# First layer's heads: the dense products of a slot stand between its scores and its turns

## The chip, the cores and the metric

One core of one Trainium2 chip runs the whole program. The metric is the device time of one execution in microseconds (us), the median of several runs. TensorE (PE) does the matrix products and the transposes; its weight loads are listed apart as PEld. VectorE (DVE), ScalarE (ACT) and GpSimd (POOL) do the rest, and SyncE (SP) issues transfers.

## The reference, cut to what matters

Four layers, each an attention part and a feed-forward part that both read the layer's normalised input. Only the attention of the first layer is touched. It has two batches of 1024 tokens, 16 query heads of 128 dimensions and 4 groups of keys and values, and it is causal:

```python
q = einsum('bsh,he->bse', x, w_q).reshape(b, sq, GROUPS, HPG, KVC)
scores = einsum('bqgpd,bkgd->bgqpk', q, k) * SCALE
scores = where(causal, scores, -inf)
probs = softmax(scores, axis=-1)
ctx = einsum('bgqpk,bkgd->bqgpd', probs, v).reshape(b, sq, HEADS * KVC)
return einsum('bse,eh->bsh', ctx, w_dense)
```

## The kernel before, in words

The function `l0_heads` runs the 16 heads one after the other, the inner ones in a hardware loop. Each engine has its own instruction list, written out by hand, and works through it in that order; the lists meet only at semaphores. Nothing plans the order: it is that of the calls in each engine's `step`.

The work of a head is 16 units. A unit is one tile of 128 queries (number t, 0 to 7, of batch b), whose scores are 128 x 128(t+1). In each batch the tiles come in the order t = 0, 1, 6, 7, 2, 3, 4, 5. Two units that follow each other are a pair. A head is 18 slots: 16 for units and two in which the queries of a coming head are projected. In a batch's half of a head these are nine slots: t=0, 1, 6, 7, then the projection, then t=2, 3, 4, 5.

A unit passes through the engines over several slots:

- its own slot: TensorE makes the scores (`scores`, L486 to L488 and the causal mask at L490) in a PSUM bank pair `sc`; DVE takes the row maximum (`row_max`, L592); ACT takes the exponential (`exp`, L682) and writes `probs`.
- two slots later: TensorE turns the probabilities (`turn_probs`, L501: transposes of 128 x 128 blocks, t+1 of them, four to a tile, two PSUM banks `tp` in turn); ACT writes the rounded high part (`high_probs`, L672, tile PTH); DVE writes the remainder (`low_probs`, L614, tile PTL).
- three slots after the pair's second unit: TensorE weighs the values (`weigh_values`, L516 to L518, into `cx`), and ACT copies the result to `ctxT` (`keep_ctx`, L690).
- four slots after the pair's second unit: TensorE multiplies `ctxT` with the output weights (`dense`, L530, plain fp32, two products that the trace shows as four records, into `outp`), and DVE adds it to the sum (`add_dense`, L624).

So a slot of TensorE's list holds scores, then turns of the unit two slots back, then, in some slots, a dense product or the weighing of values. A slot never has both a dense product and a weighing. The slots with a dense product are those of t=1, t=7, t=2 and t=4; what they turn is t=5 (six blocks), t=1 (two blocks), t=7 (eight blocks) and t=2 (three blocks). The slot after each of them has no dense product.

What TensorE waits for, by name: the turns wait for the probabilities and for a free bank (`pt_lo`, the remainder of the tile two before: `pe.wait_ge(pt_lo, NT * h + n - 1)`, L499); the weighing waits for the remainder of all its unit's tiles (`pt_lo`, L509); the dense product waits for `ctx_ready`, the copy of the context (L526), and for the sum before it (`added`, L528). ACT's list in a slot is `high_probs`, then `exp` (or `high_queries` in a projection slot), then `keep_ctx`. DVE's list in a slot is `row_max`, then `invert` and `low_probs`, then `low_queries` in a projection slot, then `add_dense`.

The two lines that set the order of a slot on TensorE after its scores:

```python
if u := unit_at(h, s, 2):
    turn_probs(*u)
if (u := unit_at(h, s, 4)) and u[1] % 2:
    dense(*u)
```

Of the kernel before, what the change touches and what calls it, by code (L numbers as in the profile page):

```python
# [217 lines left out]
def split_product(pe, out, w_hi, w_lo, x_hi, x_lo):  # L218

    terms = [(w, x, c) for c in range(DC) for w, x in ((w_hi, x_hi), (w_hi, x_lo), (w_lo, x_hi))]  # L220
    for i, (w, x, c) in enumerate(terms):
        mm = pe.matmul(out, w(c), x(c), start=(i == 0), stop=(i == len(terms) - 1))  # L222
    return mm
# [142 lines left out]
def l0_heads(nc, k, a, kd, vd, kv):  # L366
# [15 lines left out]
    with Stage(nc, "l0h") as st:  # L382
# [20 lines left out]
        def back(h, s, n):  # L403

            return (h, s - n) if s >= n else (h - 1, s - n + NS)

        def exists(h):
            return not isinstance(h, int) or 0 <= h <= LAST

        def unit_at(h, s, n):  # L410


            hh, ss = back(h, s, n)
            kind, i = SLOTS[ss]
            return (hh, i) if kind == "unit" and exists(hh) else None
# [12 lines left out]
        with nc.Block() as block:  # L428
# [29 lines left out]
            def _(pe):  # L458
                def project(h, b, bank):

                    pe.wait_ge(wlo_ready, h + 1)
                    for j in range(S // BANK):
                        tok = slice(b * S + j * BANK, b * S + (j + 1) * BANK)
                        mm = split_product(pe, bank[:, j * BANK:(j + 1) * BANK], lambda c: wq_hi[:, c, :], lambda c: wq_lo[:, c, :],
                                           lambda c: k.XH[:, c, tok], lambda c: k.XL[:, c, tok])
                        mm.then_inc(q_made, 1)

                def bank_free(h, s):
                    hh, ss = back(h, s, 2)
                    if exists(hh):  # L470
                        kind, i = SLOTS[ss]
                        if kind == "unit":
                            pe.wait_ge(probs_ready, NU * hh + i + 1)
                        elif exists(hh + 1 - i):
                            pe.wait_ge(ql_ready, 2 * hh + (3 if i == 0 else 2))

                def scores(h, s, i):
                    b, t = UNITS[i]
                    pe.wait_ge(kv.keys_here[b], h + 1)
                    pe.wait_ge(ql_ready, 2 * h + 1 + b)  # L480
                    q = slice(b * S + t * P, b * S + (t + 1) * P)
                    for lo in range(0, (t + 1) * P, BANK):
                        n = min(BANK, (t + 1) * P - lo)
                        key = slice(b * S + lo, b * S + lo + n)
                        diagonal = lo + n == (t + 1) * P
                        pe.matmul(sc[s % 2][:, lo:lo + n], QH[:, q], kv.KH[:, key], start=True, stop=False)  # L486
                        pe.matmul(sc[s % 2][:, lo:lo + n], QH[:, q], kv.KL[:, key], start=False, stop=False)
                        mm = pe.matmul(sc[s % 2][:, lo:lo + n], QL[:, q], kv.KH[:, key], start=False, stop=not diagonal)  # L488
                        if diagonal:
                            mm = pe.matmul(sc[s % 2][:, t * P:(t + 1) * P], ident[:, :], causal[:, :], start=False, stop=True)  # L490
                    mm.then_inc(scores_ready, 1)

                def turn_probs(h, i):
                    b, t = UNITS[i]
                    pe.wait_ge(probs_ready, NU * h + i + 1)
                    for j in range(TILES[i]):
                        n = FIRST_TILE[i] + j
                        if n >= 2 or not isinstance(h, int) or h > 0:
                            pe.wait_ge(pt_lo, NT * h + n - 1)  # L499
                        for kb in range(4 * j, min(4 * j + 4, t + 1)):  # L500
                            mm = pe.transpose(tp[n % 2][:, (kb - 4 * j) * P:(kb - 4 * j + 1) * P], probs[:, i % 4, kb * P:(kb + 1) * P], k.ident[:, :])  # L501
                        mm.then_inc(turned, 1)

                def weigh_values(h, i):


                    b, t = UNITS[i]
                    pair = i // 2
                    pe.wait_ge(pt_lo, NT * h + FIRST_TILE[i + 1])  # L509
                    pe.wait_ge(kv.values_here[b], h + 1)  # L510
                    if pair or not isinstance(h, int) or h > 0:
                        pe.wait_ge(ctx_ready, NPAIR * h + pair)
                    for kb in range(t + 1):
                        col = slice(0 if kb < t else P, L0_PAIR)
                        V = b * NQ + kb
                        pe.matmul(cx[:, col], kv.VH[:, V, :], PTH[:, pair % 2, kb, col], start=(kb == 0), stop=False)  # L516
                        pe.matmul(cx[:, col], kv.VH[:, V, :], PTL[:, pair % 2, kb, col], start=False, stop=False)  # L517
                        mm = pe.matmul(cx[:, col], kv.VL[:, V, :], PTH[:, pair % 2, kb, col], start=False, stop=(kb == t))  # L518
                    mm.then_inc(pv_done, 1)

                def dense(h, i):

                    pair = i // 2
                    if pair == 0:
                        pe.wait_ge(wd_loaded, 16)
                    pe.wait_ge(ctx_ready, NPAIR * h + pair + 1)  # L526
                    if pair or not isinstance(h, int) or h > 0:
                        pe.wait_ge(added, NPAIR * h + pair)  # L528
                    for j in range(2):
                        mm = pe.matmul(outp[:, j * D:(j + 1) * D], ctxT[:, pair % 2, j * P:(j + 1) * P],  # L530
                                       wd[:, ds(h, 1), :].rearrange("p a n -> p (a n)"), start=True, stop=True)
                    mm.then_inc(dense_done, 1)

                def step(h, s):
                    if exists(h):
                        kind, i = SLOTS[s]
                        if kind == "unit":
                            bank_free(h, s)
                            scores(h, s, i)
                        elif exists(h + 1 - i):  # L540
                            bank_free(h, s)
                            project(h + 1 - i, i, sc[s % 2])
                    if u := unit_at(h, s, 2):
                        turn_probs(*u)
                    if (u := unit_at(h, s, 4)) and u[1] % 2:
                        dense(*u)
                    if (u := unit_at(h, s, 3)) and u[1] % 2:
                        weigh_values(*u)

                project(0, 0, sc[1])  # L550
                pe.wait_ge(mask_here, 1)
                steps(pe, step)
                for n in range(NJ * DC):
                    j, c = divmod(n, DC)
# [2427 lines left out]
```

## Time and profile before

| | us |
|---|---|
| median of 3 runs | 3763.67 (3762.89 to 3767.64) |
| the profiled execution's own time | 3760.89 |
| its span in the trace | 3759.1 |
| TensorE busy | 3383.6 (90%) |
| DVE busy | 2424.6 (64%) |
| ACT busy | 1569.3 (42%) |
| the stage of the heads, about | 120 to 968 |

The stage of the heads takes 848 us of the span, about 52 us for a head and 26 us for a batch's half of one. The groups of instructions say what each line costs in sum; the waits say who waited for whom; the timeline of one engine in one short stretch says in which order the instructions ran, when each started, how long its record is, and in brackets how long the engine sat idle before it and what released it. A matmul's record includes the drain of its result, so records overlap: the distance from one start to the next is what a matmul occupies.

### The profile page before, as it was taken

How to read it: one execution, taken by the hardware profiler on the slowest of the kernel's cores; microseconds unless marked ns; L12 is line 12 of the kernel's file. 1: busy time of each engine (PE TensorE's matmuls, PEld its weight loads, DVE VectorE, ACT ScalarE, POOL GpSimd, SP SyncE). 2: the span in 40 equal slices, each digit the busy share in tenths (PEclk: the TensorE clock that was granted, in tenths of full speed). 3: DMA queues.
4: the chain of work that ended last, by engine and by line, in shares of the span. 5: the costliest groups of instructions: out<-in, count | busy, mean ns of one | idle time of the engine just before them, and what ended most of it. 6: DMA issues, size and time to landing. Idle time of an engine off the chain costs nothing. (4 is left out here: it accounts for less than half of the span.)

```text
span 3759.1 us, 65234 instructions
## 1 busy us (share of the span) xinstructions
PE 3383.6 (90%) x21360; PEld 2613.8 (70%) x21360; DVE 2424.6 (64%) x4499; ACT 1569.3 (42%) x2871; POOL 1181.3 (31%) x851
## 2 busy tenths in 40 slices
PE   6799999999697999999996669999769999799997
PEld 4688888888475888888883335555348887388883
DVE  3466666666424656656655778888468887488873
ACT  2355555555233444444442316666333332333332
POOL 1202020110024666666662400000014444444444
PEclk8899999999898999999998879999979999899998
DMA  3100000000101000000000502222044443144441
GB/s 111 63 3 25 3 24 3 18 10 0 35 0 45 15 18 18 16 18 18 18 8 3 199 36 82 82 82 74 12 137 117 112 114 80 44 107 116 114 98 48
DMA packets 133296, 199.97 MB, mean 53 GB/s; under 512 B 23072, under 2 KB 78240, under 8 KB 132896
## 3 DMA queue, kind: packets, MB, share of 16 engines
q1 hardware_dynamic: 127072, 190.55, 16.3%
q0 software_dynamic: 6144, 8.39, 1.4%
q8 instruction: 45, 0.74, 0.1%
q14 instruction: 35, 0.29, 0.0%
HBM read 162.06 MB, written 36.57 MB: 53 GB/s over the span
## 5 line engine op out<-in xcount | busy, mean ns | idle before, releaser
L1942 DVE TENSOR_REDUCE l2h_half<-l2h_s 128x1 f32<-128x512 f32 x512 | 337.5, 686 | 50.3 <-PE l2h_s L1844 49.3
L1929 ACT ACTIVATE l2h_PT<-l2h_s 128x1024 f32<-128x1024 f32 x256 | 248.3, 1022 | 164.9 <-PE l2h_s L1854 164.8
L592 DVE TENSOR_REDUCE l0h_negtop<-l0h_sc 128x1 f32<-128x128 f32 (+7 forms) x256 | 192.8, 753 | 191.7 <-PE l0h_sc L490 187.8
L614 DVE TENSOR_TENSOR l0h_PTL<-l0h_tp,l0h_PTH 128x512 fp32r<-128x512 f32 (+3 forms) x384 | 200.4, 549 | 122.9 <-ACT l0h_PTH L672 120.0
L672 ACT ACTIVATE l0h_PTH<-l0h_tp 128x512 fp32r<-128x512 f32 (+3 forms) x384 | 175.4, 496 | 219.1 <-PE l0h_tp L501 218.9
L1844 PE MATMUL l2h_s<-l2h_K,l2h_Q 128*128 128x512 f32 x512 | 219.1, 466 | 23.5 <-DMA l2h_K<-l_split 20.4
L682 ACT ACTIVATE l0h_probs<-l0h_sc,l0h_negtop 128x128 f32<-128x128 f32 (+7 forms) x256 | 190.3, 743 | 116.1 <-DVE l0h_negtop L592 115.1
L159 POOL TENSOR_TENSOR XN<-XN,n_rstd 128x512 f32<-128x512 f32 x32 | 39.9, 1268 | 593.7 <-DVE n_rstd L140 593.7
L568 POOL TENSOR_TENSOR l0h_wq_lo<-l0h_wq,l0h_wq_hi 128x256 fp32r<-128x256 f32 x16 | 11.8, 739 | 630.0 <-ACT l0h_wq_hi L656 630.0
L516 PE MATMUL l0h_cx<-l0h_PTH,l0a_VH 128*128 128x256 f32 (+1 forms) x640 | 184.3, 288 | 17.0 <-DVE l0h_PTL L614 16.9
L501 PE MATMUL l0h_tp<-ident,l0h_probs 128*128 128x128 f32 x1152 | 177.4, 276 | 20.7 <-DVE l0h_PTL L614 20.7
L517 PE MATMUL l0h_cx<-l0h_PTL,l0a_VH 128*128 128x256 f32 (+1 forms) x640 | 180.0, 281 | 0.0
L518 PE MATMUL l0h_cx<-l0h_PTH,l0a_VL 128*128 128x256 f32 (+1 forms) x640 | 179.5, 280 | 0.0
L1844 PEld LDWEIGHTS l2h_s<-l2h_K,l2h_Q 128*128 128x128 f32 x512 | 99.2, 195 | 113.9 <-DVE l2h_half L1942 75.3
L1854 PE MATMUL l2h_s<-l2h_Q,l2h_K 128*128 128x512 f32 x512 | 162.3, 400 | 0.0
L1138 ACT ACTIVATE l1a_kswap<-l1a_pk,l1a_bias 64x512 f32<-64x512 f32 x64 | 43.8, 685 | 278.0 <-PE l1a_pk L222 278.0
L2587 POOL TENSOR_TENSOR l3p_w_lo<-l3p_w,l3p_w_hi 128x1024 fp32r<-128x1024 f32 x34 | 80.4, 2363 | 252.1 <-ACT l3p_w_hi L2530 252.1
L486 PE MATMUL l0h_sc<-l0a_KH,l0h_QH 128*128 128x512 f32 (+3 forms) x384 | 156.9, 409 | 2.0 <-DVE l0h_QL L598 1.5
L2673 DVE TENSOR_TENSOR_SCAN l3p_table<-l3p_decb,l3p_eye 128x512 f32<-128x512 f32 x128 | 151.2, 1222 | 0.4 <-issue 0.4
L2711 DVE SCALAR_TENSOR_TENSOR l3p_state<-l3p_state,l3p_prow,l3p_dsm 128x128 f32<-128x128 f32 x192 | 146.1, 761 | 6.8
L501 PEld LDWEIGHTS l0h_tp<-ident,l0h_probs 128*128 128x128 f32 x1152 | 126.5, 141 | 34.2 <-DVE l0h_PTL L614 28.2
L2538 ACT ACTIVATE l3p_xT<-l3p_px 128x512 f32<-128x512 f32 x64 | 38.3, 598 | 263.4 <-PE l3p_px L222 263.4
(423 smaller groups left out, 9903.8 us busy)
## 6 DMA issues: line engine op xcount, KB each, us to landing
l3p_decb<-l_decays SPq DMA_DIRECT2D x128, 256.0 KB, 4.4
l3p_w<-L_w SPq DMA_DIRECT2D x34, 512.0 KB, 3.6
l2h_Q<-l_split SPq DMA_DIRECT2D x64, 256.0 KB
l2h_K<-l_split SPq DMA_DIRECT2D x64, 256.0 KB
l3p_prow<-l_decays SPq DMA_DIRECT2D x128, 128.0 KB, 3.1
l_split<-l2q_hi SPq DMA_DIRECT2D x16, 512.0 KB, 3.9
l_split<-l2q_lo SPq DMA_DIRECT2D x16, 512.0 KB, 3.8
l3p_wgu<-L_ffn_w_gate_up SPq DMA_DIRECT2D x32, 256.0 KB, 4.8
```

Source lines behind the costliest of these rows:

```text
L501: mm = pe.transpose(tp[n % 2][:, (kb - 4 * j) * P:(kb - 4 * j + 1) * P], probs[:, i % 4, kb * P:(kb + 1) * P], k.ident[:, :])
L516: pe.matmul(cx[:, col], kv.VH[:, V, :], PTH[:, pair % 2, kb, col], start=(kb == 0), stop=False)
L517: pe.matmul(cx[:, col], kv.VH[:, V, :], PTL[:, pair % 2, kb, col], start=False, stop=False)
L518: mm = pe.matmul(cx[:, col], kv.VL[:, V, :], PTH[:, pair % 2, kb, col], start=False, stop=(kb == t))
L592: dve.reduce_max(negtop[:, i % 4:i % 4 + 1], sc[s % 2][:, 0:(t + 1) * P], AX_X, negate=True).then_inc(top_ready, 1)
L614: dve.tensor_tensor(PTL[part], tp[n % 2][:, 0:m * P].rearrange("p (m n) -> p m n", m=m), PTH[part].bitcast(F32), ALU.subtract).then_inc(pt ...
L672: act.activation(PTH[:, pair % 2, 4 * j:4 * j + m, i % 2 * P:(i % 2 + 1) * P], tp[n % 2][:, 0:m * P].rearrange("p (m n) -> p m n", m=m), A ...
L682: act.activation(probs[:, i % 4, 0:(t + 1) * P], sc[s % 2][:, 0:(t + 1) * P], ACT.Exp, bias=negtop[:, i % 4:i % 4 + 1], accum_out=total[:, ...
L1844: pe.matmul(bank(slot_of(i))[:, :], Q1[:, b, t * P:(t + 1) * P], K1[:, b, z * BANK:(z + 1) * BANK], start=True, stop=True).then_inc(s1_mad ...
L1854: mm = pe.matmul(s2[kb % 2][:, z * BANK:(z + 1) * BANK], K2[:, b, kb * P:(kb + 1) * P], Q2[:, b, z * BANK:(z + 1) * BANK], start=True, sto ...
L1929: act.activation(PT[:, b, kb, :], s2[kb % 2][:, :], ACT.Exp, scale=L2_SCALE).then_inc(exped, 1)
L1942: dve.reduce_max(half[:, b, t, z:z + 1], bank(slot_of(i))[:, :], AX_X).then_inc(s1_read, 1)
```

## The change

Two statements of TensorE's `step` change places. In a slot that has a dense product, it now comes right behind the slot's scores, and the turns come behind it. No instruction is added or taken away, and the lists of DVE, ACT, GpSimd and SyncE are the same as before, word for word.

```diff
@@ -540,10 +540,10 @@
                         elif exists(h + 1 - i):
                             bank_free(h, s)
                             project(h + 1 - i, i, sc[s % 2])
+                    if (u := unit_at(h, s, 4)) and u[1] % 2:
+                        dense(*u)
                     if u := unit_at(h, s, 2):
                         turn_probs(*u)
-                    if (u := unit_at(h, s, 4)) and u[1] % 2:
-                        dense(*u)
                     if (u := unit_at(h, s, 3)) and u[1] % 2:
                         weigh_values(*u)
```

TensorE, the slot of t=2, whose turns are the eight blocks of t=7 (names: `l0h_sc` the scores' bank, `l0h_tp` the turns' bank, `l0h_outp` the dense product's bank; a leading + is a row of the changed kernel, a leading - one of the kernel before):

```order
 L488 MATMUL l0h_sc<-l0a_KH,l0h_QL 128x384
 L490 MATMUL l0h_sc<-l0h_causal,l0h_ident 128x128
+L530 MATMUL l0h_outp<-l0h_wd,l0h_ctxT 128x256 x2
 L501 MATMUL l0h_tp<-ident,l0h_probs 128x128 x8
-L530 MATMUL l0h_outp<-l0h_wd,l0h_ctxT 128x256 x2
 L486 MATMUL l0h_sc<-l0a_KH,l0h_QH 128x512
```

The eight turns now stand behind the dense product and directly ahead of the scores of t=3, after which the values of t=7 are weighed.

TensorE, the slot of t=4, whose turns are the three blocks of t=2:

```order
 L488 MATMUL l0h_sc<-l0a_KH,l0h_QL 128x128
 L490 MATMUL l0h_sc<-l0h_causal,l0h_ident 128x128
+L530 MATMUL l0h_outp<-l0h_wd,l0h_ctxT 128x256 x2
 L501 MATMUL l0h_tp<-ident,l0h_probs 128x128 x3
-L530 MATMUL l0h_outp<-l0h_wd,l0h_ctxT 128x256 x2
 L486 MATMUL l0h_sc<-l0a_KH,l0h_QH 128x512
```

The three turns moved behind the dense product; what follows them is the slot of t=5.

TensorE, the slot of t=1, whose turns are the six blocks of t=5:

```order
 L488 MATMUL l0h_sc<-l0a_KH,l0h_QL 128x256
 L490 MATMUL l0h_sc<-l0h_causal,l0h_ident 128x128
+L530 MATMUL l0h_outp<-l0h_wd,l0h_ctxT 128x256 x2
 L501 MATMUL l0h_tp<-ident,l0h_probs 128x128 x6
-L530 MATMUL l0h_outp<-l0h_wd,l0h_ctxT 128x256 x2
 L486 MATMUL l0h_sc<-l0a_KH,l0h_QH 128x512
```

Between the weighing that makes the dense product's input and the dense product there now stand only the scores of t=1.

## Rows read from the trace of the kernel before

**Rows 1.** Page: busy time of the engines over the whole span.
```profile
PE 3383.6 (90%) x21360; PEld 2613.8 (70%) x21360; DVE 2424.6 (64%) x4499; ACT 1569.3 (42%) x2871; POOL 1181.3 (31%) x851
```
**Rows 2.** Busy time by stretch: PE, PEld, DVE, ACT, POOL, granted clock, DMA share, GB/s.
```profile
120.00:968.00 848.00, 806.93 (x5401) 707.42 (x5400) 526.27 (x1093) 453.46 (x1104) 68.38 (x39) 1.00 0.03 11
```
**Rows 3.** Waits of PE, 120 to 968: us in total, times, longest us.
```profile
PE l0h_tp L501 <- DVE l0h_PTL L614: 20.7, 34, 1.0
PE l0h_cx L516 <- DVE l0h_PTL L614: 16.9, 32, 0.7
```
**Rows 4.** Waits of PE's weight loads, same stretch.
```profile
PEld l0h_cx L516 <- DVE l0h_PTL L614: 21.6, 32, 1.1
```
**Rows 5.** Timeline of PE, slots of t=7 to t=3: start, length, instruction, idle before.
```profile
417.77 0.39 PE L501 MATMUL l0h_tp<-ident,l0h_probs 128*128 128x128 f32 x2
...
422.28 0.36 PE L516 MATMUL l0h_cx<-l0h_PTH,l0a_VH 128*128 128x256 f32 x1
...
423.66 1.08 PE L501 MATMUL l0h_tp<-ident,l0h_probs 128*128 128x128 f32 x8
424.57 1.08 PE L530 MATMUL l0h_outp<-l0h_wd,l0h_ctxT 128*128 x4
...
426.99 0.39 PE L516 MATMUL l0h_cx<-l0h_PTH,l0a_VH 128*128 128x256 f32 x1 [0.56 <-DVE l0h_PTL L614]
```
**Rows 6.** Timeline of ACT, around the slot of t=2.
```profile
424.06 0.42 ACT L690 ACTIVATE l0h_ctxT<-l0h_cx 128x256 f32<-128x256 f32 x1
424.32 1.13 ACT L672 ACTIVATE l0h_PTH<-l0h_tp 128x512 fp32r<-128x512 f32 x2
```
**Rows 7.** Timeline of DVE, slot of t=2.
```profile
425.67 1.26 DVE L614 TENSOR_TENSOR l0h_PTL<-l0h_tp,l0h_PTH 128x512 fp32r<-128x512 f32 x2
```
**Rows 8.** Timeline of PE, slots of t=4 to t=0.
```profile
430.99 0.50 PE L501 MATMUL l0h_tp<-ident,l0h_probs 128*128 128x128 f32 x3
431.32 1.03 PE L530 MATMUL l0h_outp<-l0h_wd,l0h_ctxT 128*128 x4
432.00 0.58 PE L486 MATMUL l0h_sc<-l0a_KH,l0h_QH 128*128 128x512 f32 x1
...
435.33 0.33 PE L501 MATMUL l0h_tp<-ident,l0h_probs 128*128 128x128 f32 x1 [0.61 <-DVE l0h_PTL L614]
```
**Rows 9.** Timeline of ACT, slots of t=4 to t=1.
```profile
431.52 0.49 ACT L672 ACTIVATE l0h_PTH<-l0h_tp 128x384 fp32r<-128x384 f32 x1 [1.05 <-PE l0h_tp L501]
...
437.25 0.38 ACT L690 ACTIVATE l0h_ctxT<-l0h_cx 128x256 f32<-128x256 f32 x1 [0.76 <-PE l0h_cx L518]
438.09 0.87 ACT L672 ACTIVATE l0h_PTH<-l0h_tp 128x512 fp32r<-128x512 f32 x2 [0.46 <-PE l0h_tp L501]
```
**Rows 10.** Timeline of DVE, slots of t=4 to t=1.
```profile
432.04 0.56 DVE L614 TENSOR_TENSOR l0h_PTL<-l0h_tp,l0h_PTH 128x384 fp32r<-128x384 f32 x1
432.52 0.86 DVE L624 SCALAR_TENSOR_TENSOR l0h_acc<-l0h_outp,l0h_inv,l0h_acc 128x256 f32<-128x256 f32 x2
433.51 0.96 DVE L592 TENSOR_REDUCE l0h_negtop<-l0h_sc 128x1 f32<-128x768 f32 x1
434.38 0.15 DVE L605 RECIPROCAL l0h_inv<-l0h_total 128x2 f32<-128x2 f32 x1
434.58 0.69 DVE L614 TENSOR_TENSOR l0h_PTL<-l0h_tp,l0h_PTH 128x512 fp32r<-128x512 f32 x1
...
438.72 1.02 DVE L614 TENSOR_TENSOR l0h_PTL<-l0h_tp,l0h_PTH 128x512 fp32r<-128x512 f32 x2 [0.58 <-ACT l0h_PTH L672]
```
**Rows 11.** Timeline of PE, slots of t=1 and t=6.
```profile
437.45 0.83 PE L501 MATMUL l0h_tp<-ident,l0h_probs 128*128 128x128 f32 x6
...
440.30 0.36 PE L516 MATMUL l0h_cx<-l0h_PTH,l0a_VH 128*128 128x256 f32 x1
```
**Rows 12.** Timeline of PE in the last head, where turns follow a dense product directly.
```profile
940.82 1.03 PE L530 MATMUL l0h_outp<-l0h_wd,l0h_ctxT 128*128 128x256 f32 x4
941.68 0.60 PE L501 MATMUL l0h_tp<-ident,l0h_probs 128*128 128x128 f32 x4
```

## The prediction, made before the changed kernel was run

> **What bounds the kernel now.** I read the page's busy times first: TensorE is busy for 90% of the span, the next engine for 64% [rows 1]. Then the stage of the heads alone, the only one that the change touches: of 848.0 us TensorE's records cover 806.9, at a granted clock of 1.00, its 2.4 GHz level; DVE works 526.3 us, ACT 453.5 [rows 2]. So the stage ends when TensorE ends, and each us that TensorE waits there is a us of the kernel. Third, the waits: two groups carry nearly all of them, and both are for DVE's remainders of the turned probabilities: 20.7 us in 34 waits ahead of a turn, 16.9 in 32 ahead of a weighing [rows 3]. There are 32 half heads, so each wait comes once in a half. Last, the timelines of three engines over one half (848 / 32, about 26 us) show where. Wait A, 0.56 us, stands ahead of the weighing of t=7, in the slot of t=3 [rows 5]. Wait B, 0.61 us, stands ahead of the second tile of t=4's turns, in the slot of t=0 [rows 8]. Neither slot holds a dense product, so the change cannot lay a dense product over either wait. What it does is start four turns per half later, and ask for four dense inputs earlier.
>
> **What a dense product costs where it stands.** Before, the scores behind it start 0.68 us later (431.32 to 432.00 [rows 8]), but the one place in this trace where turns follow it directly, late in the last head, shows 0.86 us (940.82 to 941.68 [rows 12]). I take 0.86 as the delay of the turns and 0.68 as the lower bound. I count no change in the stream's sum: the same products run, only the neighbours change. That part is bounded below.
>
> **First place, the slot of t=2.** Ahead stands a projection slot, in which ACT's list has the rounding of the queries and only then the copy of the context: that copy starts at 424.06 and lasts 0.42, so `ctxT` is there at 424.48 [rows 6]. TensorE is through with the scores at 423.66 and starts the eight turns there; before, these covered the copy, and the dense product at 424.57 found its input ready [rows 5]. Now the dense product is asked for at 423.66 and stands some 0.87 us. Then the chain runs: dense starts at about 424.55 (the copy's end plus 0.06, the lag between DVE's end at 425.67 + 1.26 = 426.93 [rows 7] and TensorE's start at 426.99 [rows 5]), turns at 424.55 + 0.86 = 425.41, ACT's high part 0.64 later (437.45 to 438.09 [rows 9, 11]) at 426.05, DVE's remainder 0.63 later (438.09 to 438.72 [rows 9, 10]) at 426.68. DVE is free by then, since before it began this same work at 425.67 [rows 7]. The pair of remainders takes 1.16 us when ACT's pieces (1.13 for two [rows 6]) pace it, my estimate from that row, so it ends at 427.84 and the weighing of t=7 starts at 427.90 instead of 426.99: **+0.91 us**. Wait A stays about as long as it is (turns and scores are later by as much), and a new wait on `ctxT` of about 0.87 stands ahead of the dense product. With 0.68 for the dense product it is +0.73. Behind the waiting dense product TensorE's list holds the turns and the scores of t=3; ACT's next high part and DVE's next remainder wait for these.
>
> **Second place, the slot of t=4.** The dense product finds its input here: the five pieces of scores in between are long. The three turns start at 430.99 + 0.86 = 431.85 instead of 430.99 [rows 8]. ACT followed 0.53 later (431.52 [rows 9]): now 432.38. DVE followed ACT by 0.52 (432.04 [rows 10]): now 432.90. From there DVE's list goes on without a pause: the addition of the dense product 0.48 later (432.04 to 432.52), the next row maximum 0.78 after that (its 0.86 less the overlap of 0.08 that neighbours on DVE show), at 434.16 instead of 433.51; the reciprocal 0.87 on (433.51 to 434.38), at 435.03; the remainder of t=3 about 0.07 on, at 435.10 instead of 434.58 [rows 10]. That remainder is what wait B waits for, so B grows by **+0.52 us**. The cover here was 0.21 of pause ahead of the row maximum and 0.13 ahead of the remainder; 0.86 less these is the same 0.52. With 0.68 it is +0.34.
>
> **Third place, the slot of t=1.** The weighing of t=3 has just ended, and only the short scores of t=1 stand ahead of the dense product. ACT's copy starts at 437.25 and ends at 437.63 [rows 9], so the product starts at 437.69, not at 437.45: a new wait of 0.24. The six turns of t=5 start at 438.55 instead of 437.45 [rows 11], 1.10 later. ACT and DVE had idled ahead of them [rows 9, 10], so the chain moves one to one: remainders at 438.72 + 1.10 = 439.82, done after 1.02 [rows 10] at 440.84, weighing of t=5 at 440.90 instead of 440.30 [rows 11]: **+0.60 us**; at least the +0.24 of the first wait, if the rest were hidden. With 0.68, +0.42.
>
> **Fourth place, the slot of t=7.** The turns of t=1 (two blocks) are followed by a projection before the values are weighed: 4.51 us from the turns at 417.77 to the weighing at 422.28 [rows 5], where the chain from the turns to the remainder needs about 0.64 + 0.63 and the remainder itself. Cost zero; the projection is the cover. Without it the price would be the 0.86 at most.
>
> **The rule weighed.** TensorE's weight loads show no load that passed a waiting product: the loads of the weighing waited for the remainders too, 21.6 us in 32 waits [rows 4], though their weights, the values, do not depend on these. So I count no load of the turns as done during the new waits. The Trainium skill, TensorE: Matmul & The Clock Gate, section The mechanism, says that TensorE pulls weight loads ahead of matmuls in flight. By that the first load of the turns could lie in the new wait of the first and third place; at an estimated 0.1 us each (a turn's spacing of 0.91/8) the sum would be some 6 us smaller. The trace rather speaks against it here.
>
> **The sum.** 0.91 + 0.52 + 0.60 = 2.03 us for a half. I count 31 halves: the first half head lacks a third place, and the last half of the last head has no projection ahead of its first. 31 x 2.03 = 63 us. Against the profiled execution, 3760.9 us, that gives 3824; the median of the runs is 2.8 higher, so 3763.7 + 63 = 3827 us. Bounds: with 0.68 for the dense product 0.73 + 0.34 + 0.42 = 1.49, or 46 us, 3810; above, a slot that loses another 0.05 where neighbours changed (four per half, 128 in all) adds 6 us, 3833. The same 0.05 below zero would take 6 off.
>
> **Rivals.**
> - *Only the first place costs.* If the lists of ACT and DVE hide the second and third (0.13 + 0.21 of pause at the second, the scores of t=6 at the third), 31 x 0.91 = 28 us remain: 3792. For it: the third place has the scores of t=6 between turns and weighing. Against: the weighing already starts at 440.30 with DVE done at 439.74, 0.56 of slack against 1.10. Chance 0.10.
> - *Faster.* A dense product is dear for what follows: the next scores start at 0.68, but turns at 0.86, so the product's tail lies on its successor. If turns, whose loads are short, cover 0.13 of that tail better than scores do, TensorE's stream shrinks by 128 x 0.13 = 17 us: 3747. It decides only if the three places together cost less than 4 x 0.13 = 0.52 us a half; I count 2.03, and rows 12 show no such cover. Chance 0.04.
> - *No change.* The dense product could be asked for early without delay if its input were always there, and the turns' delay fall into waits A and B: 3764. Against: the copy's end at 424.48 stands 0.82 behind 423.66. Chance 0.03.
> - *Dearer.* If the late exponentials also hold back the score banks (that of t=4 stands behind the late high part on ACT, and the scores of t=0 want its bank), or ACT's copies fall behind, another 0.4 us a half: 3840. Chance 0.06.
>
> **The numbers.** The forecast has 0.77; its own range is 3810 to 3833. The range from 3792 to 3836 takes in the first rival and leaves out the other three, 0.13. A difference under 0.2% (7.5 us) is about what a measurement can't tell from none. Slower by more: 0.77 + 0.10 + 0.06 = 0.93; within: 0.03; faster: 0.04.
>
> **What would show it.** In the trace after: waits of TensorE for ACT's `ctxT`, near 0.87 us ahead of the dense product of the slot of t=2 and near 0.24 in that of t=1, 35 us in all, where before there was next to none; waits ahead of t=4's second tile of turns near 1.13 instead of 0.61, about 36 us in all; waits ahead of the weighing not shorter than 16.9 and up by some 11 (the third place's 0.36). The stage near 911 us instead of 848. Nothing else may move. I am wrong if the turns start earlier than 0.7 us behind the dense product, or if the waits for `ctxT` are missing.

## The result and the profile after

The changed kernel takes 3846.82 us (median, 3842.23 to 3848.37) against 3765.65 for the kernel before in the same runs: a ratio of 1.021, with a 95% interval of 1.0193 to 1.0228. It is slower by 81 us. The prediction had 3827 us, slower by 63, with a range up to 3836: the sign, the three places and their order of size were right, but the sum was too small by 18 us, and the time lies 11 us above the range. One execution of the kernel before in a later group of runs (4480.49 us, at a mean granted clock of 0.72 where the others have 0.95) is left out of every comparison.

Nearly all of the time went in the stage of the heads: 80.2 us there, as measured below, of the 81 between the medians. The page's first part and the stage's row of busy time by stretch (columns as in [rows 2]):

```profile
PE 3418.4 (89%) x21360; PEld 2626.0 (68%) x21360; DVE 2424.4 (63%) x4499; ACT 1563.1 (41%) x2871; POOL 1183.1 (31%) x851
120.00:1052.00 932.00, 839.95 (x5408) 718.58 (x5407) 528.05 (x1096) 446.45 (x1104) 68.18 (x39) 1.00 0.03 10
```

The same instructions ran, the granted clock stayed at 1.00, the 2.4 GHz level, and DVE's and ACT's work in the stage is the same within 7 us. TensorE's records cover 33 us more (839.95 against 806.93), though the products are the same. Most of that is waiting out of sight: a record includes the drain, so a wait that begins under the record before it is counted as idle only from that record's end. Against [rows 3], TensorE's waits in the stage (us in total, times, longest):

```profile
PE l0h_tp L501 <- DVE l0h_PTL L614: 32.3, 33, 1.5
PE l0h_cx L516 <- DVE l0h_PTL L614: 27.4, 33, 1.6
PE l0h_outp L530 <- ACT l0h_ctxT L690: 26.0, 46, 0.8
```

Both old waits grew (20.7 to 32.3 and 16.9 to 27.4), and a third appeared, of the dense product for the copy of the context. These rows add up to 48 us more than before; with the 33 us under records that is about what the stage lost.

One half head of the changed kernel, in the order of time. TensorE's timeline (start, length, instruction, idle before), to be laid beside [rows 5, 8, 11]:

```profile
452.00 0.39 PE L486 MATMUL l0h_sc<-l0a_KH,l0h_QH 128*128 128x384 f32 x1
...
453.51 1.13 PE L530 MATMUL l0h_outp<-l0h_wd,l0h_ctxT 128*128 x4 [0.71 <-ACT l0h_ctxT L690]
454.48 1.04 PE L501 MATMUL l0h_tp<-ident,l0h_probs 128*128 128x128 f32 x8
...
457.09 0.38 PE L516 MATMUL l0h_cx<-l0h_PTH,l0a_VH 128*128 128x256 f32 x1 [0.80 <-DVE l0h_PTL L614]
...
461.08 1.08 PE L530 MATMUL l0h_outp<-l0h_wd,l0h_ctxT 128*128 x4
462.00 0.49 PE L501 MATMUL l0h_tp<-ident,l0h_probs 128*128 128x128 f32 x3
...
465.98 0.33 PE L501 MATMUL l0h_tp<-ident,l0h_probs 128*128 128x128 f32 x1 [0.84 <-DVE l0h_PTL L614]
...
468.03 0.23 PE L490 MATMUL l0h_sc<-l0h_causal,l0h_ident 128*128 128x128 bf16 x1
468.43 1.12 PE L530 MATMUL l0h_outp<-l0h_wd,l0h_ctxT 128*128 x4 [0.17 <-ACT l0h_ctxT L690]
469.39 0.82 PE L501 MATMUL l0h_tp<-ident,l0h_probs 128*128 128x128 f32 x6
...
471.41 0.33 PE L501 MATMUL l0h_tp<-ident,l0h_probs 128*128 128x128 f32 x1
471.74 0.39 PE L516 MATMUL l0h_cx<-l0h_PTH,l0a_VH 128*128 128x256 f32 x1
```

ACT's timeline in the same half, to be laid beside [rows 6, 9]:

```profile
453.04 0.41 ACT L690 ACTIVATE l0h_ctxT<-l0h_cx 128x256 f32<-128x256 f32 x1
455.12 1.09 ACT L672 ACTIVATE l0h_PTH<-l0h_tp 128x512 fp32r<-128x512 f32 x2 [1.66 <-PE l0h_tp L501]
...
467.90 0.39 ACT L690 ACTIVATE l0h_ctxT<-l0h_cx 128x256 f32<-128x256 f32 x1 [0.61 <-PE l0h_cx L518]
```

And DVE's, beside [rows 7, 10]:

```profile
455.75 1.29 DVE L614 TENSOR_TENSOR l0h_PTL<-l0h_tp,l0h_PTH 128x512 fp32r<-128x512 f32 x2 [1.00 <-ACT l0h_PTH L672]
...
465.25 0.67 DVE L614 TENSOR_TENSOR l0h_PTL<-l0h_tp,l0h_PTH 128x512 fp32r<-128x512 f32 x1
...
470.66 1.02 DVE L614 TENSOR_TENSOR l0h_PTL<-l0h_tp,l0h_PTH 128x512 fp32r<-128x512 f32 x2 [1.87 <-ACT l0h_PTH L672]
```

Slot of t=2: the copy ends at 453.04 + 0.41 = 453.45, the dense product starts at 453.51, the turns only at 454.48; DVE, which before was late itself, now idles 1.00 us until ACT has a high part for it. From the first score of t=2 to the weighing of t=7 it is 457.09 - 452.00 = 5.09 us. Slot of t=4: the product needs no wait, the turns start 0.92 behind it, and t=4's second tile of turns waits until 465.98 for a remainder that DVE starts at 465.25. Slot of t=1: the copy starts at 467.90, the dense product at 468.43, the turns at 469.39, the weighing of t=5 at 471.74. The product could have followed the mask's product (468.03) by some 0.06, so it waits 0.34 us, of which the timeline shows the 0.17 behind that record's end.

### The profile page after: what moved, and what is told of

Its sections match the earlier page's. It is cut to its first block and busy times, and to the rows that moved or that the text cites. A ratio compares the mean times of both kernels' runs of the same rounds, so it can differ in the third digit from the quotient of the medians.

```text
span 3845.1 us, 65234 instructions
## 1 busy us (share of the span) xinstructions
PE 3418.4 (89%) x21360; PEld 2626.0 (68%) x21360; DVE 2424.4 (63%) x4499; ACT 1563.1 (41%) x2871; POOL 1183.1 (31%) x851
## 5 line engine op out<-in xcount | busy, mean ns | idle before, releaser
L516 PE MATMUL l0h_cx<-l0h_PTH,l0a_VH 128*128 128x256 f32 (+1 forms) x640 | 185.0, 289 | 27.5 <-DVE l0h_PTL L614 27.4
L501 PE MATMUL l0h_tp<-ident,l0h_probs 128*128 128x128 f32 x1152 | 176.8, 276 | 32.5 <-DVE l0h_PTL L614 32.3
L501 PEld LDWEIGHTS l0h_tp<-ident,l0h_probs 128*128 128x128 f32 x1152 | 136.7, 141 | 58.6 <-DVE l0h_PTL L614 40.1
L530 PE MATMUL l0h_outp<-l0h_wd,l0h_ctxT 128*128 (+1 forms) x512 | 141.5, 399 | 26.9 <-ACT l0h_ctxT L690 26.0
L486 PE MATMUL l0h_sc<-l0a_KH,l0h_QH 128*128 128x512 f32 (+3 forms) x384 | 147.6, 384 | 2.1 <-DVE l0h_QL L598 1.5
```

## The experiments

The stage below is measured from the first scores of the first head to the start of the last addition of a dense product, so that what lies ahead of the heads does not enter. For the kernel before these are 124.67 and 964.1, 839.4 us; for the changed one 126.05 and 1045.6, 919.6 us: +80.2. "Over before" is the difference of the medians within the runs that share their runs of the kernel before. The stage is read from one traced execution of each kernel, so the two columns can differ by some us.

| kernel | median | over before | ratio, 95% | stage over before |
|---|---|---|---|---|
| changed | 3846.82 | +81.2 | 1.0193 to 1.0228 | +80.2 |
| only in the slot of t=2 | 3807.97 | +41.3 | 1.0089 to 1.0123 | +36.4 |
| only in the slot of t=4 | 3780.84 | +14.2 | 1.0032 to 1.0068 | +17.9 |
| only in the slot of t=1 | 3794.97 | +28.3 | 1.0054 to 1.0088 | +24.9 |
| only in the slot of t=7 | 3767.14 | +0.5 | 0.9995 to 1.0015 | +2.0 |
| changed, without the context's wait | 3809.07 | +40.3 | 1.0088 to 1.0122 | +45.9 |
| changed, copy ahead of the queries | 3819.28 | +50.5 | 1.0118 to 1.0152 | +52.8 |
| changed, addition one slot later | 3832.87 | +64.1 | 1.0151 to 1.0185 | +63.7 |
| before, dense product of t=4 in the slot of t=0 | 3752.97 | -15.8 | 0.9951 to 0.9976 | -14.6 |
| before, DVE exchanged in the slot of t=2 | 3750.31 | -14.1 | 0.9950 to 0.9972 | -14.7 |
| changed, DVE exchanged in the slot of t=2 | 3845.56 | +81.2 | 1.0197 to 1.0230 | +80.1 |
| before, both of these | 3735.67 | -28.7 | 0.9903 to 0.9931 | -29.1 |

**One place at a time.** Two theories: each place pays for itself, through the waits that the prediction followed; or a dense product is simply dearer in the stream behind scores than behind turns, which would cost alike in all four slots. The edit, here for the slot of t=2 (slots 5 and 14; the others are 7 and 16, 1 and 10, 3 and 12):

```diff
+                    early = s in (5, 14)
+                    if early and (u := unit_at(h, s, 4)) and u[1] % 2:
+                        dense(*u)
                     if u := unit_at(h, s, 2):
                         turn_probs(*u)
-                    if (u := unit_at(h, s, 4)) and u[1] % 2:
+                    if not early and (u := unit_at(h, s, 4)) and u[1] % 2:
                         dense(*u)
```

> The dense product ahead of the turns only in the slot of t=2, the other three slots as before. Theory of waits (each place pays for itself, by the wait on the context's copy and the later chain): the trace after shows 5.09 us from the scores of t=2 to the weighing of t=7 against 3.99 before, so +1.1 a half, 31 halves: +34 us, stage of the heads about 882. The prediction's own size was +28. Rival, a dearer stream (a dense product costs more behind scores than behind turns, alike in all four slots): a quarter of 81, +20.

> Only in the slot of t=4. Theory of waits: DVE's list (remainder of t=2, addition, row maximum, remainder of t=3) moves, and the wait ahead of t=4's second tile of turns grows by 0.52 to 0.55: 32 halves, +17 us, no new wait on the context. Rival, a dearer stream: +20, and it would show between the dense product and the scores of t=5, not at the second tile.

> Only in the slot of t=1. Theory of waits: +0.6 (the prediction) to +0.8 (read from the trace after) a half: +19 to +25 us; a wait on the context's copy of 0.2 to 0.4 ahead of the dense product and a new wait ahead of the weighing of t=5. Rival, a dearer stream: +20 with no wait ahead of the weighing.

> Only in the slot of t=7, where a projection follows the turns. Theory of waits: 0 to +3 us (the trace after shows 0.05 to 0.09 a half). Rival, a dearer stream: +20, as in the others. This run tells the two apart.

The four stages add up to 36.4 + 17.9 + 24.9 + 2.0 = 81.2 us, against 80.2 for the whole change (the medians to 84.3, against 81.2). They are unlike, and the fourth, where only the neighbours change and a projection covers the rest, costs 2.0 us of the stage, 0.06 a half, and nothing that the medians can tell. So a dense product that costs alike in all four slots is out, and so is the rival that the first place alone would cost. TensorE's waits, in the kernel with the slot of t=2 alone, then with t=4 alone, then with t=1 alone:

```profile
PE l0h_cx L516 <- DVE l0h_PTL L617: 26.6, 33, 0.9
PE l0h_outp L530 <- ACT l0h_ctxT L693: 23.2, 32, 0.8
PE l0h_tp L501 <- DVE l0h_PTL L617: 20.4, 33, 1.0
```

```profile
PE l0h_tp L501 <- DVE l0h_PTL L617: 32.5, 34, 1.5
PE l0h_cx L516 <- DVE l0h_PTL L617: 17.2, 32, 0.7
```

```profile
PE l0h_cx L516 <- DVE l0h_PTL L617: 18.0, 32, 1.6
PE l0h_outp L530 <- ACT l0h_ctxT L693: 3.4, 16, 0.5
```

With t=2 alone, the wait for the copy and the growth of the wait ahead of the weighing are there, and the turns' wait is as before. With t=4 alone it is the turns' wait that grows, by 12 us in 34 waits, and nothing new waits for the context.

With t=1 alone, the new wait ahead of the weighing of t=5 that was expected is not in the list (18.0 us against 16.9 before), and no wait there is what the rival had said of this slot. The timelines of the changed kernel tell more. Ahead of that weighing stands a single turn, and the weighing starts 0.33 us behind it (471.41 to 471.74); in the kernel before it was 0.04 (440.26 below, to 440.30 [rows 11]):

```profile
440.26 0.28 PE L501 MATMUL l0h_tp<-ident,l0h_probs 128*128 128x128 f32 x1
```

DVE's remainders end at 470.66 + 1.02 = 471.68, and the weighing follows 0.06 later. So there is a wait of 0.29, and the turn's record of 0.33 hides all of it. The kernel with t=1 alone has the same 0.33.

**The wait for the context taken away.** In the changed kernel the dense product reads the identity, which is always there:

```diff
-                    pe.wait_ge(ctx_ready, NPAIR * h + pair + 1)
...
-                        mm = pe.matmul(outp[:, j * D:(j + 1) * D], ctxT[:, pair % 2, j * P:(j + 1) * P],
+                        mm = pe.matmul(outp[:, j * D:(j + 1) * D], k.ident[:, :],
```

> The changed kernel, but the dense product takes the identity in place of the context as its stationary operand and does not wait for the copy (so the attention's result is left out). Theory of waits: the waits for the copy go, and what they delayed: the first place falls from +1.10 to about +0.2 a half, the third from +0.80 to about +0.45, the second stays at +0.55, the fourth at 0.05 to 0.09: 1.3 a half, about +41 us over the kernel before, 40 below the changed one. If the waits for the copy were only a symptom and the later turns alone were the price, little would go: over +65. The start of the turns behind the dense product should fall from 0.97 to 0.92 or less if the context's weight load is what makes the difference.

It is 40.3 us over before, 41 below the changed kernel (the stage: 45.9, 34 below): about half of the loss came from asking for the context too early. The rest comes with the later turns. TensorE's timeline around the slot of t=2:

```profile
440.28 0.39 PE L486 MATMUL l0h_sc<-l0a_KH,l0h_QH 128*128 128x384 f32 x1
...
440.92 1.08 PE L529 MATMUL l0h_outp<-l0h_wd,ident 128*128 x4
441.84 1.04 PE L501 MATMUL l0h_tp<-ident,l0h_probs 128*128 128x128 f32 x8
...
444.52 0.38 PE L516 MATMUL l0h_cx<-l0h_PTH,l0a_VH 128*128 128x256 f32 x1 [0.88 <-DVE l0h_PTL L613]
```

From the scores of t=2 to the weighing it is 4.24 us, 0.85 less than in the changed kernel; and the turns start 0.92 us behind the dense product, not 0.97.

**The copy ahead of the queries.** In the changed kernel, ACT's list of a projection slot:

```diff
                         elif exists(h + 1 - i):
+                            if (u := unit_at(h, s, 3)) and u[1] % 2:
+                                keep_ctx(*u)
                             high_queries(2 * h + (3 if i == 0 else 2), i, sc[s % 2])
```

(with the call at the slot's end left out there)

> The changed kernel, but ACT copies the context ahead of rounding the queries in the two projection slots of a head. Theory of waits: at the first place the copy ends about 0.8 us earlier, the dense product waits 0.1 instead of 0.87; the queries' remainder and with it the row maximum and the remainder of t=7 on DVE come about 0.5 later, so about 0.6 of the 0.8 is gained: 31 halves, 15 to 20 us below the changed kernel, +62 to +66 over before. If ACT's order is not what holds the copy back: no difference to the changed kernel.

It gains 27 us of the stage (31 by the medians), more than the 15 to 20 expected, and the wait for the context falls from 26.0 us in 46 waits to this row:

```profile
PE l0h_outp L530 <- ACT l0h_ctxT L690: 3.4, 16, 0.5
```

So the order of ACT's list is what held the first place's copy back. I had charged the later rounding of the queries with 0.2 us a half on DVE; the trace shows that DVE's remainder of t=7 still starts 0.63 behind ACT's high part (443.45 to 444.08), so that delay is hidden. ACT's timeline there, then DVE's:

```profile
441.41 0.38 ACT L690 ACTIVATE l0h_ctxT<-l0h_cx 128x256 f32<-128x256 f32 x1
...
443.45 1.09 ACT L672 ACTIVATE l0h_PTH<-l0h_tp 128x512 fp32r<-128x512 f32 x2 [0.68 <-PE l0h_tp L501]
```

```profile
444.08 1.29 DVE L614 TENSOR_TENSOR l0h_PTL<-l0h_tp,l0h_PTH 128x512 fp32r<-128x512 f32 x2
```

**The addition one slot later.** In the changed kernel, DVE's list:

```diff
+                    if (u := unit_at(h, s, 5)) and s in (8, 17) and u[1] % 2:
+                        add_dense(*u)
-                    if (u := unit_at(h, s, 4)) and u[1] % 2:
+                    if (u := unit_at(h, s, 4)) and s not in (7, 16) and u[1] % 2:
                         add_dense(*u)
```

> The changed kernel, but DVE adds the dense product of the slot of t=4 one slot later, behind the remainder of t=3. Theory for the second place (the chain runs through DVE's list, whose addition of 0.78 stands ahead of the row maximum): the +0.55 there vanishes, 32 halves: 17 us below the changed kernel. If the chain there runs through ACT instead (high part, exponential, high part): no difference.

The stage falls by 16.5 us, and TensorE's waits ahead of the turns from 32.3 to 16.0 us (the row below, from the waits). So the second place's chain runs through DVE's list, as the prediction had it.

```profile
PE l0h_tp L501 <- DVE l0h_PTL L614: 16.0, 33, 1.0
```

**Can a dense product between scores and turns be worth something?** Where the turns would wait anyway, it should. In the kernel before, on TensorE (and likewise the addition on DVE):

```diff
+                    if (u := unit_at(h, s, 6)) and s in (0, 9) and u[1] % 2:
+                        dense(*u)
                     if u := unit_at(h, s, 2):
                         turn_probs(*u)
-                    if (u := unit_at(h, s, 4)) and u[1] % 2:
+                    if (u := unit_at(h, s, 4)) and s not in (7, 16) and u[1] % 2:
                         dense(*u)
```

> The kernel before, but the dense product of the slot of t=4 is made two slots later on TensorE and DVE, in the slot of t=0 between its scores and its turns. There the wait of 0.61 for the remainder of t=3 stands with nothing to cover it. Theory of waits: the product covers it, the turns' second tile waits no more: 32 x 0.6 = 19 us below the kernel before. If turns that start later always cost by the length of the product: no gain, or up to +10 us.

It is faster than before, by 0.24 to 0.49%, and wait B is gone: 0.7 us in 3 waits are left of 20.7 in 34. The row of the wait, then TensorE's timeline in the slot of t=0:

```profile
PE l0h_tp L501 <- DVE l0h_PTL L616: 0.7, 3, 0.3
```

```profile
428.06 1.08 PE L530 MATMUL l0h_outp<-l0h_wd,l0h_ctxT 128*128 x4
428.98 0.71 PE L501 MATMUL l0h_tp<-ident,l0h_probs 128*128 128x128 f32 x5
```

The five turns of t=4 run in one piece behind the product. This is the order of the change (scores, dense product, turns), in a slot where the turns had to wait anyway and with an input that is long there. The gain is 4 to 5 us less than the wait that it removed. About 4 us of it are lost in the slot of t=1: its turns and its dense product take 0.71 and 0.75 us to the next start (431.35, 432.06, 432.81) instead of 0.66 and 0.68 (437.45, 438.11, 438.79 before), 0.12 a half. What makes them longer was not tried.

**What holds wait A.** DVE's list has the row maximum of t=2 ahead of the remainders of t=7. Exchanged, in the slot of t=2 only:

```diff
-                    if kind == "unit" and exists(h):
+                    if s not in (5, 14) and kind == "unit" and exists(h):
                         row_max(h, s, i)
...
                         low_probs(*u)
+                    if s in (5, 14) and exists(h):
+                        row_max(h, s, i)
```

> The kernel before, but in the slot of t=2 DVE makes the remainders of t=7 ahead of the row maximum of t=2. Wait A ahead of the weighing of t=7 is then held by DVE's list no more: the remainders can start at 425.13 instead of 425.67, so 0.5 of the 0.56 goes: 32 x 0.5 = 16 us below before. If A is set by the turns and ACT instead: no difference.

> The same exchange on DVE, in the changed kernel. There, by the theory of waits, the remainders of t=7 wait for turns that start 1.8 us later and DVE idles 1.0 us ahead of them, so the exchange gives nothing to TensorE: within 3 us of the changed kernel, +80 over before (the row maximum of t=2 comes later, which costs nothing while its bank is not wanted). If DVE's list still set wait A in the changed kernel: 16 us below it.

In the kernel before, the exchange takes 14.1 us off and wait A falls from 16.9 us to 0.7. In the changed kernel it does nothing (+81.2 over before, with it and without), and the wait stays at 27.5: there the remainders wait for the late turns, and DVE idles 1.47 us ahead of them. The same wait, by name and place, has another cause in the two kernels. The rows are the wait ahead of the weighing with the exchange, in the kernel before and then in the changed one, and last the timeline of DVE's remainders in the changed one:

```profile
PE l0h_cx L516 <- DVE l0h_PTL L614: 0.7, 1, 0.7
```

```profile
PE l0h_cx L516 <- DVE l0h_PTL L614: 27.5, 33, 1.6
```

```profile
454.68 1.29 DVE L614 TENSOR_TENSOR l0h_PTL<-l0h_tp,l0h_PTH 128x512 fp32r<-128x512 f32 x2 [1.47 <-ACT l0h_PTH L674]
```

**Both together,** on the kernel before:

> The kernel before with both: the dense product of the slot of t=4 made in the slot of t=0 between scores and turns, and DVE's exchange in the slot of t=2. If the two waits of a half are separate, the gains add: 15 + 16 = 31 us below before, 3735. If one wait only moves to the other: 16.

The gains add: 3735.67 us, ratio 0.9917 (0.9903 to 0.9931). That is 28.7 us, where the two alone give 15.8 + 14.1 = 29.9. It is the fastest of all the kernels here. The two waits of a half head were separate.

## Why the prediction fell short

Right were: that no dense product covers waits A or B; that three of the four slots pay, by the chains named; that the fourth is covered; that ACT's list holds back the first place's copy, and DVE's addition the second place.

Of the waits that it named, the one ahead of the turns came to 32.3 us (about 36 said) and the one for the context to 26.0 (35 said; the trace counts no idle while the records of the scores' last products run out). The one ahead of the weighing came to 27.4, where about 28 was said, but that was luck: the prediction let wait A stay and put the growth into the third place. With t=1 alone the row is 18.0, with t=2 alone 26.6. It was wait A that grew, from 0.56 to 0.80 in the timelines, and the third place's wait is hidden under a record.

What failed is the size of the terms, and first the step "What a dense product costs where it stands": 0.86 us as the delay of the turns. In the half head shown, the four slots cost 1.10, 0.55, 0.80 and 0.05 us, 2.50 in all, where the sum had 0.91, 0.52, 0.60 and 0, 2.03. (Over the 32 halves the mean distances from one weighing to the next grew by 1.14, 0.54, 0.74 and 0.09, also 2.50, 80 us.) Each of the first three begins with the delay of the turns by a dense product, taken as 0.86 from [rows 12]; it measured 0.97 in the first place, 0.92 in the second, 0.96 in the third. That alone is 0.11 + 0.06 + 0.10 = 0.27 of the missing 0.47.

The rest: in the first place the pair of remainders took 1.29 us (455.75) instead of 1.16, which is 0.13. The 1.16 was taken from ACT's pace, but DVE's own work on this pair already took 1.26 before, in [rows 7], with ACT's pieces finished at 424.32 + 1.13 = 425.45, ahead of its start. In the third place the copy's end reached the product after 0.14 instead of 0.06 (467.90 + 0.39 = 468.29, against 468.43), which is 0.08, and the fourth slot's 0.05 (4.56 from 446.71 to 451.27, against 4.51 before) was put at nothing. Smaller differences, as of a copy in the first place that ended 0.03 earlier, take the remaining 0.06 off.

Why 0.86 did not carry over can be read from the weight loads. The rows are the load of the dense product in the last head of the kernel before, then the loads in the first and second place of the changed one:

```profile
940.71 0.73 PEld L530 LDWEIGHTS l0h_outp<-l0h_wd,l0h_ctxT 128*128 128x128 f32 x4
```

```profile
453.51 0.73 PEld L530 LDWEIGHTS l0h_outp<-l0h_wd,l0h_ctxT 128*128 128x128 f32 x4 [0.84 <-ACT l0h_ctxT L690]
454.26 1.01 PEld L501 LDWEIGHTS l0h_tp<-ident,l0h_probs 128*128 128x128 f32 x8
...
461.02 0.74 PEld L530 LDWEIGHTS l0h_outp<-l0h_wd,l0h_ctxT 128*128 128x128 f32 x4
```

In the row that I took the price from, the load began at 940.71, 0.11 us ahead of its product, beneath two turns. Behind the scores it begins 0.06 ahead (461.02 to 461.08), since the mask's product there is short (0.06 to the next start); behind a wait it begins with the product, because the context is the stationary operand and can't be loaded before it exists. Lead and delay add up to 0.97 or 0.98 each time: 0.11 + 0.86, 0.06 + 0.92, 0 + 0.97. The kernel without the wait agrees: 0.92 in the place where the changed kernel has 0.97.

The kernel with the copy ahead of the queries parts the lead from the wait. In its slot of t=2 the product waits no more (it starts 0.07 behind the mask's product at 441.79), but the copy ends only at 441.41 + 0.38 = 441.79, so the load has a lead of just 0.01, and the turns follow after 0.96. Its load, then its product and turns:

```profile
441.85 0.73 PEld L530 LDWEIGHTS l0h_outp<-l0h_wd,l0h_ctxT 128*128 128x128 f32 x4
```

```profile
441.86 1.12 PE L530 MATMUL l0h_outp<-l0h_wd,l0h_ctxT 128*128 x4
442.82 1.04 PE L501 MATMUL l0h_tp<-ident,l0h_probs 128*128 128x128 f32 x8
```

The kernel before showed the same of the scores behind a dense product. In the slot of t=4 the load leads by 0.11 and the scores follow after 0.68 (431.32 to 432.00 [rows 8]); in the slot of t=2 it leads by 0.05 and they follow after 0.74 (424.57 [rows 5] to 425.31). The two loads, then those scores:

```profile
431.21 0.73 PEld L530 LDWEIGHTS l0h_outp<-l0h_wd,l0h_ctxT 128*128 128x128 f32 x4
```

```profile
424.52 0.73 PEld L530 LDWEIGHTS l0h_outp<-l0h_wd,l0h_ctxT 128*128 128x128 f32 x4
```

```profile
425.31 0.58 PE L486 MATMUL l0h_sc<-l0a_KH,l0h_QH 128*128 128x512 f32 x1
```

So the trace before already held a price that moved with the lead. That the uncovered load is the cause is read from these sums; no run was made to vary the lead alone.

The rule of the Trainium skill that was weighed (TensorE: Matmul & The Clock Gate, section The mechanism: loads are pulled ahead of matmuls in flight) was rightly not counted. The turns' first load in the first place comes at 454.26, behind the dense product's at 453.51: no load of the turns passed the waiting product. The changed order even loses the small lead that the rule describes.

The rival "dearer" had a mechanism that did occur: the late exponential of t=4 held back the score bank of t=0, so that in this half 0.62 us (463.45 to 464.07 in the trace after) instead of 0.36 (433.31 to 433.67 before) lie between the turns of t=3 and those scores. But the wait ahead of t=4's second tile stands right behind and ends with DVE's remainder at 465.25 + 0.67 = 465.92, which does not hang on those scores; read from the rows, this cost nothing. Its 3840 came nearer to the time, for another reason.

My range was too narrow for this: its upper end allowed 0.05 us for each of four slots, while the price of the moved product alone, taken from a single place with another neighbour, was uncertain by 0.11 in each of three chains, some 10 us by itself.

## What to carry to other kernels

On an engine that works in order, a product can be moved ahead of other work only as far as its input is early: before, the turns had covered the copy that the product needs, and moving it paid for that copy, and then for every chain that started with the turns. Look which instruction at that moment starts the longest chain on the other engines and issue it first; put the product that nobody waits for where the engine idles. And take the price of an instruction from a place with the neighbours that it will have: the same product delayed its follower by 0.86, 0.92 or 0.97 us.

## What was not expected of the hardware

In these traces the lead of a weight load over its product, from 0 to 0.11 us by what stands ahead of it, comes off the delay that a plain fp32 product gives to its follower. And ACT's copy reached TensorE 0.06 us after its end in the first place and 0.14 in the third, for the same instruction. It is not the place that decides: in the half ahead of the one shown the first place has 0.15 (424.51 + 0.41 = 424.92, to 425.07) and the third 0.05 (439.27 + 0.38 = 439.65, to 439.70). What makes the difference stays open.
